# Where a five-layer graph network builds its one-hot matrices, and in which order TensorE uses them

## The chip, the cores and the metric

The kernel runs on one core of a Trainium2 chip. The metric is the time of one execution in microseconds (us) on the device. Before the change the median of three runs is 13644.97 us (13634.25 to 13649.05).

## The reference, cut to what matters

There are 6250 nodes of 64 features and 200000 edges, sorted by destination node. Four graph blocks follow each other; the first has two attention layers, so there are five message-passing layers, called a to e below. Each computes, in its own variant (one or four heads; layers d and e also use one of 8 edge types):

```
score = f(source row[src] , destination row[dst] , edge features)     # one value per edge and head
alpha = exp(score - max over the edges of dst) / sum over the edges of dst
out   = segment_sum(alpha * source row[src], dst)
```

Layers a and b add `edge_attr @ We` (64 features per edge) inside the score, layer c takes the sum of two scalars per head, and layers d and e take dot products. Between the layers stand small dense products and layer norms over the 6250 nodes.

## The kernel before, in words

`prepare` (line 180 and on) computes things that all layers share. Every edge gets the rank of its destination among the destinations that occur; because edges are sorted, the 128 edges of a tile touch only a few neighbouring ranks, so a tile needs one window number and, for each edge, a small rank relative to that window (`rel`, below 256). Then `layer` runs five times: `tables` makes the source rows (to HBM) and the destination rows (`dstW`, in SBUF as three bf16 parts), `stream` walks over all edges, `merge` and `finish` do the rest. Nearly all the time is in `stream`.

`stream` works in groups of 8 tiles of 128 edges, 196 groups in all, and four groups make a chunk (49 chunks). Each engine has its own program, a list of steps, one step per group `u`; engines run in order and meet only at semaphores. The loop over steps is written out for 12 steps (`RING`), and repeats. The two one-hot matrices of a group are:

- `hot` (made by VectorE, `onehot`, L973): 256 ranks on partitions and columns by 1024 edges; it compares a row of relative ranks, loaded by SyncE's queue and spread over the partitions, with the partition's number. TensorE uses it in `expand` to spread destination rows to edges (48 matmuls, six per tile, L1174, and in layers a and b four more for the edge features, L1169).
- `ahot` (made by VectorE, `collect_hot`, L1071): edges on partitions by 256 ranks for each of 8 tiles; it compares `rel` with a table of column numbers, `rankX`. TensorE uses it in `collect` to add the weighted messages by rank (48 matmuls, L1189).

In step `u` the engines do the following; `k = u - LAG` (6 groups behind, 8 in layer d) is the group that is being weighted, and `r = u % 4` is the place in the chunk.

- GpSimd gathers the 1024 source rows of a group with eight indirect DMAs (L914), up to 12 groups ahead of the weighting. SyncE loads indices, ranks, edge features and the chunk's masks.
- VectorE, in this order: `flush(k-2)` adds two PSUM banks to `accS` (L966, waits for `collect(k-2)`); `onehot(u+2)`; the third bf16 part of `k-1` (L1127, signals `low`); where r = 1 `highest_links` (L1009 to L1011); `weigh(k)` (L1062, waits for `alpha` of its chunk), `collect_hot(k)` (L1071), a remainder (L1139); where r = 0 `highest` (L1001 to L1003, the segment maximum by scans, waits for `turned`); where r = 1 `highest_all` (L1018 to L1023, waits for `gaveC`); `score(u)` (L1093 to L1112, waits for `expand(u)` and for the gather).
- TensorE: where r = 1 `give_ends` (L1196), where r = 2 the transposition of the exponentials (L1215); `expand(u+1)`; where r = 0 the transposition of the chunk's scores (`turned`, L1226); where r = 1 `give_carry` (L1203); then `collect(k-1)`, which waits for `low` of `k-1` and for two zeroed PSUM banks.
- ScalarE: sets each PSUM bank to zero after its flush (L929); copies `alpha` from PSUM where r = 2 (L932; in layer d where r = 3, L944); rounds two bf16 parts (L936, L938); where r = 1 the exponential (L941).

Layer d normalises in the stream as well: `total` (r = 2, before `weigh`), `total_links` (r = 2, before the score, waits for a second `give_ends` that TensorE issues after `expand`) and `total_all` (L1048 to L1054, r = 3, before `weigh`, waits for a `give_carry` that TensorE issues before `expand`); its `alpha` needs a matmul that TensorE issues after `expand` of r = 3.

Of the kernel before, what the change touches and what calls it, by code (L numbers as in the profile page):

```python
# [20 lines left out]
ALU = mybir.AluOpType  # L21
# [117 lines left out]
def build(nc, t, out, nlayers=5):  # L139
    with ExitStack() as ctx:  # L140
# [3 lines left out]
        def dram(name, shape, dt=F32):  # L144
# [50 lines left out]
def prepare(nc, t, m, d):  # L195

    with ExitStack() as ctx:
# [68 lines left out]

        MADE = 22

        with nc.Block() as block:
# [25 lines left out]
            def _(g):  # L295
# [18 lines left out]
                for h in range(4):  # L314
# [7 lines left out]
                                base=0, pattern=[[1, P]], channel_multiplier=-1).then_inc(made, 1)  # L322
                g.iota(m["rankX"][:, :, :], pattern=[[1, 2 * P], [0, GROUP]], base=0, channel_multiplier=0,
                       allow_small_or_imprecise_dtypes=True).then_inc(made, 1)
# [3 lines left out]
                       allow_small_or_imprecise_dtypes=True).then_inc(made, 1)  # L328
                g.iota(m["pid"][:, :], pattern=[[P, 2]], base=0, channel_multiplier=1,
                       allow_small_or_imprecise_dtypes=True).then_inc(made, 1)  # L330
# [458 lines left out]
def stream(nc, t, m, d, i, spec, table, dstW):  # L789
# [8 lines left out]
    with ExitStack() as ctx:  # L798
# [12 lines left out]
        hot = [sb(f"hot{s}", [P, 2, GE], BF16) for s in range(2)]  # L811
        ahot = [sb(f"ahot{s}", [P, 2 * P, GROUP], BF16) for s in range(2)]
        mid = [sb(f"mid{s}", [P, GROUP, D]) for s in range(2)]
# [15 lines left out]
        if i == 3:  # L829
# [12 lines left out]
        psA = [ps(f"psA{s}") for s in range(2)]  # L842
        psX, psY = ps("psX"), ps("psY")

# [3 lines left out]
        masked = [sem(f"masked{s}") for s in range(3)]  # L848
        hots, made, took, scored, sch, xch, ready, blank, wl, pch, sub, past = (
            sem(n) for n in ("hots", "made", "took", "scored", "sch", "xch", "ready", "blank", "wl", "pch", "sub", "past"))  # L850
        turned, ended, gaveE, carried, gaveC, lowered, exped, backed, alphad = (
# [22 lines left out]
        with nc.Block() as block:  # L874
# [44 lines left out]
            def _(a):  # L919
                a.wait_ge(ready, 1)  # L920
                for h in range(2):
                    a.activation(psA[h][:, 0:FW * CW], zero[:, :], ACT.Copy).then_inc(zeroed, 1)

                def step(it, s):
                    u, c, r, xc, xs, xq, k, ks = places(it, s)
# [4 lines left out]
                    if i != 3 and r == 2 and within(xc, CHUNKS):  # L930
                        a.wait_ge(backed, xc + 1)
                        a.activation(alpha[xs][:, :, :].rearrange("p h t -> p (h t)"), psY[:, 384:384 + R], ACT.Copy).then_inc(alphad, 1)  # L932
                    if within(k, GROUPS):
# [8 lines left out]
                    if i == 3 and r == 3 and within(xc, CHUNKS):  # L942
                        a.wait_ge(backed, xc + 1)
                        a.activation(alpha[xs][:, 0, :], psY[:, 384:384 + CT], ACT.Copy).then_inc(alphad, 1)  # L944
                rounds(a, step, END)

            @block.vector
            def _(v):
                v.memset(zero[:, :], 0.0).then_inc(ready, 1)
                if i <= 1:  # L950
                    v.memset(we[:, :], 0.0).then_inc(blank, 1)
                v.memset(accS[:, :, :], 0.0).then_inc(xch, 1)
                v.memset(tk[:, :, :], -BIG).then_inc(xch, 1)
                if i == 3:
                    v.memset(tk1[:, :, :], 0.0).then_inc(xch, 1)
                FIRST = 3 if i == 3 else 2
                v.wait_ge(xch, FIRST)

                def flush(k, ks):

                    windows = load_windows(nc, m["win"], k * GROUP, GROUP, mybir.EngineType.DVE, KR - 1)
                    for h in range(2):
# [3 lines left out]
                        v.tensor_tensor(at, at, psA[h][:, 0:FW * CW].rearrange("p (w f) -> p w f", f=CW), ALU.add).then_inc(flushed, 1)  # L966

                def onehot(it, s):
                    g = it * RING + s
                    v.wait_ge(fed[s % 4], it * (3 * FEED) + (s // 4) * FEED + FEED)  # L970
                    wait(v, made, g - 1)
# [22 lines left out]
                given = psY[0:1, 0:2 * (P + 1)].rearrange("a (x n) -> a x n", x=2)[:, :, 0:R - 1]  # L994

# [18 lines left out]
                def highest_all(xc, xs):  # L1014

                    link = linker(xc, 3)
                    v.wait_ge(gaveC, xc + 1)
                    v.tensor_copy(carry[:, :], psY[0:R, 258:260]).then_inc(sub, 1)  # L1018
# [25 lines left out]
                def total_all(xc, xs):  # L1044

                    link = linker(xc, 10)
                    v.wait_ge(gaveC2, xc + 1)
                    v.tensor_copy(carry[:, :], psY[0:R, 258:260]).then_inc(sub, 1)  # L1048
                    v.wait_ge(sub, xc * 2 + 2)
# [64 lines left out]
                def step(it, s):  # L1114
                    u, c, r, xc, xs, xq, k, ks = places(it, s)
                    live = within(xc, CHUNKS)
                    if within(k - 2, GROUPS):
                        flush(k - 2, (ks - 2) % RING)
                    if within(u + 2, GROUPS):
                        if known(u):  # L1120
                            onehot((u + 2) // RING, (u + 2) % RING)
                        else:
                            onehot(it if s + 2 < RING else it + 1, (s + 2) % RING)
                    if within(k - 1, GROUPS):
# [21 lines left out]
                    if within(u, GROUPS):  # L1146
                        score(it, s)
                onehot(0, 0)
                onehot(0, 1)
                rounds(v, step, END)  # L1150

            @block.tensor
            def _(pe):
# [25 lines left out]
                def collect(k, ks):  # L1179
# [3 lines left out]
                    for h in range(2):  # L1183
                        pe.wait_ge(zeroed, k * 2 + (h + 1))
                        for j in range(FL * h, FL * h + FL):
                            w = windows[j]
                            for a in range(2):
                                for part in range(3):
                                    last = pe.matmul(sums[h][a][:, bass.ds(w, 1), :], ahot[ks % 2][:, a * P:(a + 1) * P, j],  # L1189
                                                     parts[ks % 3][:, part, j, :], start=False, stop=False, skip_group_check=True)  # L1190
                        last.then_inc(summed, 1)

                def give_ends(sem_in, value, sem_out):
                    pe.wait_ge(sem_in, value)
                    pe.sem_inc(past, 1)
                    pe.transpose(psY[0:1, 0:R], ends[:, 1:2], m["ident"][0:R, 0:R])  # L1196
                    pe.transpose(psY[0:1, P:P + R], ends[:, 0:1], m["ident"][0:R, 0:R]).then_inc(sem_out, 1)

                def give_carry(sem_in, value, sem_out):
                    pe.wait_ge(sem_in, value)  # L1200
                    pe.sem_inc(past, 1)
                    for x in range(2):
                        last = pe.transpose(psY[0:R, 258 + x:259 + x], car[0:1, x, 0:R], m["ident"][0:1, 0:1])  # L1203
                    last.then_inc(sem_out, 1)

                def step(it, s):
                    u, c, r, xc, xs, xq, k, ks = places(it, s)
                    live = within(xc, CHUNKS)
                    if r == 1 and live:
                        wait(pe, alphad, xc)  # L1210
                        give_ends(ended, xc + 1, gaveE)
                    if i != 3 and r == 2 and live:
                        pe.wait_ge(exped, xc + 1)
                        pe.sem_inc(past, 1)
                        pe.transpose(psY[:, 384:384 + R], Ex[:, :], m["ident"][0:R, 0:R]).then_inc(backed, 1)  # L1215
                    if i == 3 and r == 3 and live:
# [14 lines left out]
                    if i == 3 and r == 3 and live:  # L1231
                        pe.wait_ge(normed, xc + 1)
                        pe.matmul(psY[:, 384:384 + CT], Al[:, :], m["quart"][:, :], start=True, stop=True).then_inc(backed, 1)
# [413 lines left out]
```

## Time and profile before

| what | value |
|---|---|
| median of the runs | 13644.97 us |
| the profiled execution | 13576.47 us, its span 13574.4 us |
| TensorE matmuls | 10504.2 us busy (77%) |
| VectorE | 8519.3 us (63%) |
| ScalarE | 2406.7 us (18%) |
| GpSimd | 9220.1 us (68%) |
| mean granted TensorE clock | 0.573 of full |
| DMA | 912.63 MB, 67 GB/s |

The shares are means over the whole span. The five `stream` stretches fill some 11,080 us of it, `prepare` the first 660 us, and the rest lies between the layers. Inside a stretch every group takes some 11.3 us, so a row of the timeline repeats 196 times with small differences. The chain of waits covers only the last few per cent of the span, so the stretches have to be read from the timeline.

### The profile page before, as it was taken

How to read it: one execution, taken by the hardware profiler on the slowest of the kernel's cores; microseconds unless marked ns; L12 is line 12 of the kernel's file. 1: busy time of each engine (PE TensorE's matmuls, PEld its weight loads, DVE VectorE, ACT ScalarE, POOL GpSimd, SP SyncE). 2: the span in 40 equal slices, each digit the busy share in tenths (PEclk: the TensorE clock that was granted, in tenths of full speed). 3: DMA queues.
4: the chain of work that ended last, by engine and by line, in shares of the span. 5: the costliest groups of instructions: out<-in, count | busy, mean ns of one | idle time of the engine just before them, and what ended most of it. 6: DMA issues, size and time to landing. Idle time of an engine off the chain costs nothing. (4 is left out here: it accounts for less than half of the span.)

```text
span 13574.4 us, 346433 instructions
## 1 busy us (share of the span) xinstructions
PE 10504.2 (77%) x102671; PEld 8732.6 (64%) x102672; DVE 8519.3 (63%) x15786; ACT 2406.7 (18%) x4954; POOL 9220.1 (68%) x8386
## 2 busy tenths in 40 slices
PE   2388888857888888488888857888888578888872
PEld 1377777746777777377777735777777357777762
DVE  7567777755777777355555544777777446666664
ACT  0011212111111122022222211111111112222220
POOL 0177777756777776577777735777777257777761
PEclk9855556555555555555555555555555555555555
DMA  0333333323333332222222223232222233333320
GB/s 16 84 75 71 73 73 73 73 42 75 72 72 73 73 71 57 39 55 54 55 54 55 54 54 106 77 78 77 77 78 72 69 96 78 78 78 78 78 64 11
DMA packets 771899, 912.63 MB, mean 67 GB/s; under 512 B 400125, under 2 KB 447616, under 8 KB 769760
## 3 DMA queue, kind: packets, MB, share of 16 engines
q0 software_dynamic: 267232, 390.16, 15.0%
q1 hardware_dynamic: 503008, 498.92, 13.0%
q8 instruction: 1216, 19.92, 0.6%
q14 instruction: 443, 3.63, 0.1%
HBM read 791.99 MB, written 96.35 MB: 65 GB/s over the span
## 5 line engine op out<-in xcount | busy, mean ns | idle before, releaser
L914 POOL DMA_INDIRECT bs_gat<-table_b,bs_idx x1568 | 1750.7, 1117 | 506.5 <-issue 477.5
L914 POOL DMA_INDIRECT ds_gat<-table_d,ds_idx x1568 | 1749.3, 1116 | 506.7 <-issue 506.7
L914 POOL DMA_INDIRECT as_gat<-table_a,as_idx x1568 | 1740.9, 1110 | 506.6 <-issue 477.5
L914 POOL DMA_INDIRECT es_gat<-table_e,es_idx x1568 | 1725.7, 1101 | 505.6 <-issue 505.6
L914 POOL DMA_INDIRECT cs_gat<-table_c,cs_idx x1568 | 1731.0, 1104 | 491.0 <-issue 491.0
L1174 PE MATMUL ds_psM<-dstW_d,ds_hot 128*128 x9408 | 1252.7, 232 | 194.4 <-DVEq L1107 72.2
L1174 PE MATMUL es_psM<-dstW_e,es_hot 128*128 x9408 | 1253.5, 226 | 175.9 <-issue 65.3
L1174 PE MATMUL cs_psM<-dstW_c,cs_hot 128*128 x9408 | 1232.0, 183 | 182.3 <-DVEq L1100 68.9
L1174 PEld LDWEIGHTS ds_psM<-dstW_d,ds_hot 128*128 128x128 bf16 x9408 | 972.2, 103 | 481.6 <-issue 241.1
L1174 PEld LDWEIGHTS es_psM<-dstW_e,es_hot 128*128 128x128 bf16 x9408 | 962.6, 102 | 480.8 <-issue 224.4
L1174 PEld LDWEIGHTS cs_psM<-dstW_c,cs_hot 128*128 128x128 bf16 x9408 | 967.5, 103 | 473.0 <-issue 223.3
L1174 PE MATMUL as_psM<-dstW_a,as_hot 128*128 x9408 | 997.9, 227 | 4.0
L1174 PE MATMUL bs_psM<-dstW_b,bs_hot 128*128 x9408 | 987.2, 230 | 5.0
L1174 PEld LDWEIGHTS as_psM<-dstW_a,as_hot 128*128 128x128 bf16 x9408 | 861.9, 114 | 182.3 <-issue 9.5
L1174 PEld LDWEIGHTS bs_psM<-dstW_b,bs_hot 128*128 128x128 bf16 x9408 | 862.2, 116 | 176.7 <-issue 12.3
L1189 PE MATMUL bs_psA<-bs_parts,bs_ahot 128*128 128x65 bf16 x9408 | 614.1, 251 | 181.1 <-issue 126.0
L1189 PE MATMUL as_psA<-as_parts,as_ahot 128*128 128x65 bf16 x9408 | 614.4, 251 | 180.6 <-issue 127.5
L1189 PE MATMUL cs_psA<-cs_parts,cs_ahot 128*128 128x68 bf16 x9408 | 613.6, 253 | 174.8 <-issue 161.2
L1189 PE MATMUL es_psA<-es_parts,es_ahot 128*128 128x68 bf16 x9408 | 612.8, 251 | 168.1 <-issue 144.4
L1189 PEld LDWEIGHTS as_psA<-as_parts,as_ahot 128*128 128x128 bf16 x9408 | 588.8, 167 | 211.0 <-issue 210.9
L1189 PEld LDWEIGHTS bs_psA<-bs_parts,bs_ahot 128*128 128x128 bf16 x9408 | 588.5, 167 | 211.3 <-issue 211.2
L1189 PEld LDWEIGHTS cs_psA<-cs_parts,cs_ahot 128*128 128x128 bf16 x9408 | 588.0, 168 | 201.0 <-issue 201.0
(758 smaller groups left out, 17937.2 us busy)
## 6 DMA issues: line engine op xcount, KB each, us to landing
as_rank<-rel_d SPq DMA_DIRECT2D x196, 256.0 KB
as_ea<-in_eaT SPq DMA_DIRECT2D x196, 256.0 KB
bs_rank<-rel_d SPq DMA_DIRECT2D x196, 256.0 KB
bs_ea<-in_eaT SPq DMA_DIRECT2D x196, 256.0 KB
cs_rank<-rel_d SPq DMA_DIRECT2D x196, 256.0 KB, 3.2
ds_rank<-rel_d SPq DMA_DIRECT2D x196, 256.0 KB, 3.3
es_rank<-rel_d SPq DMA_DIRECT2D x196, 256.0 KB, 3.4
table_e<-et_st SPq DMA_DIRECT2D x49, 544.0 KB, 2.7
```

Of the source, the lines that this page charges most:

```text
L914: g_.indirect_dma_start(gat[s][:, j, :], None, table, bass.IndirectOffsetOnAxis(ap=idxS[s][:, j:j + 1].bitcast(U32), axis=0)).then_inc(got ...
L1174: last = pe.matmul(o, hot[s % 2][:, a, j * P:(j + 1) * P], dstAt[a][part][:, bass.ds(w, 1), :], start=(a == part == 0 and i > 1), stop=(a ...
L1189: last = pe.matmul(sums[h][a][:, bass.ds(w, 1), :], ahot[ks % 2][:, a * P:(a + 1) * P, j], parts[ks % 3][:, part, j, :], start=False, stop ...
```

## The change: what it does

1. `hot` moves from VectorE to ScalarE. Instead of one compare per half, ScalarE computes `Square(rank - p)` and then `Relu(1 - square)`: four activations of 128x1024 for a group instead of two VectorE compares. They stand at the end of ScalarE's step, for group `u+2`, and signal the same semaphore.
2. `ahot` is made by eight `tensor_scalar` compares of 128x256, one per tile, which read the column numbers from PSUM (`psI`, fp32) and the tile's ranks as a per-partition scalar (so `rel` becomes fp32). The layout becomes tile by tile. It was one `tensor_tensor` of 128x2048 bf16 in SBUF.
3. `psY` gives its bank to `psI`, and what was in `psY` moves to other columns of `psX`. The wait on `alphad` moves from `give_ends` (r = 1) to the transposition of the scores (r = 0).
4. In TensorE's step `collect(k-1)` comes first; it was last.

```diff
-            rel=sb("rel", [P, TILES], BF16),
+            rel=sb("rel", [P, TILES]),
-            rankX=sb("rankX", [P, 2 * P, GROUP], BF16),
-            pid=sb("pid", [P, 2]),
+            iota=sb("iota", [P, 2 * P]),
+            pidN=sb("pidN", [P, 2]), one=sb("one", [P, 1]),
...
             @block.scalar
+                def onehot(it, s):
+                    g = it * RING + s
+                    a.wait_ge(fed[s % 4], it * (3 * FEED) + (s // 4) * FEED + FEED)
+                    wait(a, made, g - 1)
+                    wait(a, hots, g)
+                    for x in range(2):
+                        a.activation(off[:, x, :], rank[s % 4][:, :], ACT.Square, bias=m["pidN"][:, x:x + 1]).then_inc(apart, 1)
+                    for x in range(2):
+                        a.wait_ge(apart, g * 2 + (x + 1))
+                        last = a.activation(hot[s % 2][:, x, :], off[:, x, :], ACT.Relu, bias=m["one"][:, 0:1], scale=-1.0)
+                    last.then_inc(hots, 1)
                 def step(it, s):
...
                     if i == 3 and r == 3 and within(xc, CHUNKS):
                         a.wait_ge(backed, xc + 1)
-                        a.activation(alpha[xs][:, 0, :], psY[:, 384:384 + CT], ACT.Copy).then_inc(alphad, 1)
+                        a.activation(alpha[xs][:, 0, :], psX[:, 256:256 + CT], ACT.Copy).then_inc(alphad, 1)
+                    if within(u + 2, GROUPS):
+                        onehot((u + 2) // RING, (u + 2) % RING)
...
             @block.vector
+                v.tensor_copy(psI[:, 0:2 * P], m["iota"][:, :]).then_inc(xch, 1)
...
-                def onehot(it, s):
-                    for a in range(2):
-                        last = v.tensor_scalar(hot[s % 2][:, a, :], rank[s % 4][:, :], m["pid"][:, a:a + 1], None, ALU.is_equal)
-                    last.then_inc(hots, 1)
...
-                    v.tensor_tensor(ahot[ks % 2][:, :, :], over(m["rel"][:, bass.ds(k * GROUP, GROUP)], 1, [P, 2 * P, GROUP]),
-                                    m["rankX"][:, :, :], ALU.is_equal).then_inc(ahots, 1)
+                    for j in range(GROUP):
+                        last = v.tensor_scalar(ahot[ks % 2][:, j, :], psI[:, 0:2 * P], m["rel"][:, bass.ds(k * GROUP + j, 1)], None, ALU.is_equal)
+                    last.then_inc(ahots, 1)
...
             @block.tensor
                 def step(it, s):
+                    if within(k - 1, GROUPS):
+                        collect(k - 1, (ks - 1) % RING)
                     if r == 1 and live:
-                        wait(pe, alphad, xc)
                         give_ends(ended, xc + 1, gaveE)
...
                     if r == 0 and live:
                         pe.wait_ge(scored, xc * CG + CG)
-                        wait(pe, lowered, xc)
+                        wait(pe, alphad, xc)
                         pe.transpose(psX[0:R, 0:P], sc[xs][:, :, :].rearrange("p h t -> p (h t)"), m["ident"][:, :]).then_inc(turned, 1)
...
-                    if within(k - 1, GROUPS):
-                        collect(k - 1, (ks - 1) % RING)
```

## Rows read from the trace of the kernel before

**Rows 1.** Stretches by engine (us, then busy us of each): second and fifth layer.

```profile
3157.00:5384.00 2227.00, 1911.77 (x20331) 1677.43 (x20332) 1576.08 (x2835) 429.81 (x852) 1749.52 (x1567) 0.57 0.33 73
...
10968.00:13171.00 2203.00, 1901.20 (x18768) 1558.97 (x18768) 1400.44 (x2642) 446.01 (x852) 1725.00 (x1568) 0.57 0.32 78
```

**Rows 2.** The gathers, one tile (min/median/max ns), first layer.

```profile
L914 POOL DMA_INDIRECT as_gat<-table_a,as_idx x1568: 940/946/3140, 657.1 to 2874.6; - x196
```

**Rows 3.** The page, costliest groups: the same gathers (mean ns, idle before).

```profile
L914 POOL DMA_INDIRECT as_gat<-table_a,as_idx x1568 | 1740.9, 1110 | 506.6 <-issue 477.5
```

**Rows 4.** Timeline (start, length in us), TensorE, first layer.

```profile
2023.80 0.79 PE L1169 MATMUL as_psM<-as_we,as_ea 128*128 128x128 f32 x2 [4.46 <-issue]
...
2030.51 0.37 PE L1226 MATMUL as_psX<-ident,as_sc 128*32 128x128 f32 x1 [0.19 <-issue]
2031.70 3.12 PE L1189 MATMUL as_psA<-as_parts,as_ahot 128*128 128x65 bf16 x48 [0.82 <-issue]
...
2034.94 0.79 PE L1169 MATMUL as_psM<-as_we,as_ea 128*128 128x128 f32 x2
...
2041.41 0.21 PE L1203 MATMUL as_psY<-ident,as_car 1*32 1x1 f32 x2
2042.64 3.12 PE L1189 MATMUL as_psA<-as_parts,as_ahot 128*128 128x65 bf16 x48 [1.01 <-issue]
```

**Rows 5.** Timeline, VectorE, the same stretch.

```profile
2027.02 1.22 DVE L1071 TENSOR_TENSOR as_ahot<-rel,rankX 128x2048 bf16<-128x2048 bf16 x1
...
2031.04 0.41 DVE L1001 TENSOR_TENSOR_SCAN as_A<-as_mk,as_psX 32x128 f32<-32x128 bf16 x1 [2.19 <-PE as_psX L1226]
...
2032.04 0.69 DVE L1093 TENSOR_TENSOR as_mid<-as_psM,as_gat 128x512 f32<-128x512 f32 x1
...
2035.38 0.49 DVE L966 TENSOR_TENSOR as_accS<-as_accS,as_psA 128x325 f32 x1 [0.36 <-issue]
...
2036.50 1.02 DVE L973 TENSOR_SCALAR as_hot<-as_rank,pid 128x1024 bf16<-128x1024 bf16 x2
2037.44 0.69 DVE L1127 TENSOR_TENSOR as_parts<-as_res,as_parts 128x520 bf16<-128x520 f32 x1
2038.05 0.20 DVE L1009 TENSOR_TENSOR as_tk<-as_lk,as_psY 1x62 f32<-1x62 f32 x1
...
2038.54 0.66 DVE L1062 TENSOR_TENSOR as_wtd<-as_gat,as_alpha 128x520 f32<-128x520 f32 x1
...
2041.66 0.15 DVE L1018 COPY as_carry<-as_psY 32x2 f32<-32x2 f32 x1 [0.71 <-PE as_psY L1203]
...
2042.98 0.67 DVE L1093 TENSOR_TENSOR as_mid<-as_psM,as_gat 128x512 f32<-128x512 f32 x1
```

**Rows 6.** Timeline, VectorE, third layer.

```profile
6630.68 0.18 DVE L1099 TENSOR_TENSOR cs_red<-cs_psM,cs_gat 128x32 f32<-128x32 f32 x1
...
6632.03 0.51 DVE L966 TENSOR_TENSOR cs_accS<-cs_accS,cs_psA 128x340 f32 x1 [0.80 <-PE cs_psA L1189]
```

**Rows 7.** Timeline, VectorE, fourth layer.

```profile
9220.39 0.69 DVE L1103 TENSOR_TENSOR ds_mid<-ds_psM,ds_gat 128x512 f32<-128x512 f32 x1 [2.36 <-DMA ds_gat<-table_d,ds_idx]
...
9223.10 0.49 DVE L966 TENSOR_TENSOR ds_accS<-ds_accS,ds_psA 128x320 f32 x1 [1.05 <-issue]
...
9229.55 0.40 DVE L1039 TENSOR_TENSOR ds_tkO<-ds_lkO,ds_psY 1x254 f32<-1x254 f32 x1
...
9230.33 0.39 DVE L1041 TENSOR_TENSOR_SCAN ds_car<-ds_lkO,ds_tkO 1x128 f32<-1x128 f32 x1
...
9236.92 0.14 DVE L1048 COPY ds_carry<-ds_psY 128x2 f32<-128x2 f32 x1
...
9239.22 0.68 DVE L1062 TENSOR_TENSOR ds_wtd<-ds_gat,ds_alpha 128x512 f32<-128x512 f32 x1
```

**Rows 8.** Groups by line, ScalarE (busy us, mean ns).

```profile
L929 ACT ACTIVATE cs_psA<-cs_zero 128x340 f32<-128x340 f32 x392 | 179.4, 458 | 1058.2 <-DVE cs_accS L966 1058.2
...
L938 ACT ACTIVATE cs_parts<-cs_res 128x544 bf16<-128x544 f32 x196 | 128.7, 656 | 203.1 <-DVE cs_res L1139 203.1
...
L941 ACT ACT_TABLE_LOAD x4 | 5.1, 1283 | 0.1
```

**Rows 9.** Groups by line, VectorE, operands in PSUM.

```profile
L966 DVE TENSOR_TENSOR as_accS<-as_accS,as_psA 128x325 f32 x392 | 193.5, 494 | 165.4 <-issue 94.3 <-DVE as_accS L966 36.7 <-PE as_psA L1189 33.8
...
L712 DVE COPY bt_st<-bt_psA 128x64 f32<-128x64 f32 x49 | 11.0, 225 | 39.3 <-DMA table_b<-bt_st 38.3 <-PE bt_psD L784 1.0
```

More of the change, by code:

```diff
@@ L265, in prepare @@
         LOADS = 10
-        MADE = 22
+        MADE = 23
         with nc.Block() as block:
@@ L322, in _ @@
                                 base=0, pattern=[[1, P]], channel_multiplier=-1).then_inc(made, 1)
-                g.iota(m["rankX"][:, :, :], pattern=[[1, 2 * P], [0, GROUP]], base=0, channel_multiplier=0,
+                g.iota(m["iota"][:, :], pattern=[[1, 2 * P]], base=0, channel_multiplier=0,
                        allow_small_or_imprecise_dtypes=True).then_inc(made, 1)
@@ L328, in _ @@
                        allow_small_or_imprecise_dtypes=True).then_inc(made, 1)
-                g.iota(m["pid"][:, :], pattern=[[P, 2]], base=0, channel_multiplier=1,
+                g.memset(m["one"][:, :], 1.0).then_inc(made, 1)
+                g.iota(m["pidN"][:, :], pattern=[[-P, 2]], base=0, channel_multiplier=-1,
                        allow_small_or_imprecise_dtypes=True).then_inc(made, 1)
@@ L811, in stream @@
         hot = [sb(f"hot{s}", [P, 2, GE], BF16) for s in range(2)]
-        ahot = [sb(f"ahot{s}", [P, 2 * P, GROUP], BF16) for s in range(2)]
+        off = sb("off", [P, 2, GE], BF16)
+        ahot = [sb(f"ahot{s}", [P, GROUP, 2 * P], BF16) for s in range(2)]
         mid = [sb(f"mid{s}", [P, GROUP, D]) for s in range(2)]
@@ L842, in stream @@
         psA = [ps(f"psA{s}") for s in range(2)]
-        psX, psY = ps("psX"), ps("psY")
+        psX, psI = ps("psX"), ps("psI")
         fed = [sem(f"fed{s}") for s in range(4)]
@@ L848, in stream @@
         masked = [sem(f"masked{s}") for s in range(3)]
-        hots, made, took, scored, sch, xch, ready, blank, wl, pch, sub, past = (
-            sem(n) for n in ("hots", "made", "took", "scored", "sch", "xch", "ready", "blank", "wl", "pch", "sub", "past"))
+        hots, made, took, scored, sch, xch, ready, blank, wl, pch, sub, past, apart = (
+            sem(n) for n in ("hots", "made", "took", "scored", "sch", "xch", "ready", "blank", "wl", "pch", "sub", "past", "apart"))
         turned, ended, gaveE, carried, gaveC, lowered, exped, backed, alphad = (
@@ L931, in step @@
                         a.wait_ge(backed, xc + 1)
-                        a.activation(alpha[xs][:, :, :].rearrange("p h t -> p (h t)"), psY[:, 384:384 + R], ACT.Copy).then_inc(alphad, 1)
+                        a.activation(alpha[xs][:, :, :].rearrange("p h t -> p (h t)"), psX[:, 256:256 + R], ACT.Copy).then_inc(alphad, 1)
                     if within(k, GROUPS):
@@ L943, in step @@
                         a.wait_ge(backed, xc + 1)
-                        a.activation(alpha[xs][:, 0, :], psY[:, 384:384 + CT], ACT.Copy).then_inc(alphad, 1)
+                        a.activation(alpha[xs][:, 0, :], psX[:, 256:256 + CT], ACT.Copy).then_inc(alphad, 1)
+                    if within(u + 2, GROUPS):
+                        if known(u):
+                            onehot((u + 2) // RING, (u + 2) % RING)
+                        else:
+                            onehot(it if s + 2 < RING else it + 1, (s + 2) % RING)
+                onehot(0, 0)
+                onehot(0, 1)
                 rounds(a, step, END)
@@ L955, in _ @@
                     v.memset(tk1[:, :, :], 0.0).then_inc(xch, 1)
-                FIRST = 3 if i == 3 else 2
+                FIRST = 4 if i == 3 else 3
                 v.wait_ge(xch, FIRST)
@@ L966, in flush @@
                         v.tensor_tensor(at, at, psA[h][:, 0:FW * CW].rearrange("p (w f) -> p w f", f=CW), ALU.add).then_inc(flushed, 1)
-                def onehot(it, s):
-                    g = it * RING + s
-                    v.wait_ge(fed[s % 4], it * (3 * FEED) + (s // 4) * FEED + FEED)
-                    wait(v, made, g - 1)
-                    for a in range(2):
-                        last = v.tensor_scalar(hot[s % 2][:, a, :], rank[s % 4][:, :], m["pid"][:, a:a + 1], None, ALU.is_equal)
-                    last.then_inc(hots, 1)
                 XL = {0: 5, 1: 5, 2: 5, 3: 13, 4: 5}[i]
@@ L993, in neighbours @@
                     return take.rearrange("a (x n) -> a x n", x=2)[:, :, 0:R - 1]
-                given = psY[0:1, 0:2 * (P + 1)].rearrange("a (x n) -> a x n", x=2)[:, :, 0:R - 1]
+                given = psX[0:1, P:P + 2 * (P + 1)].rearrange("a (x n) -> a x n", x=2)[:, :, 0:R - 1]
                 def highest(xc, xs, xq):
@@ L1017, in highest_all @@
                     v.wait_ge(gaveC, xc + 1)
-                    v.tensor_copy(carry[:, :], psY[0:R, 258:260]).then_inc(sub, 1)
+                    v.tensor_copy(carry[:, :], psX[0:R, 400:402]).then_inc(sub, 1)
                     v.wait_ge(sub, (xc + 1) * (2 if i == 3 else 1) - (1 if i == 3 else 0))
@@ L1047, in total_all @@
                     v.wait_ge(gaveC2, xc + 1)
-                    v.tensor_copy(carry[:, :], psY[0:R, 258:260]).then_inc(sub, 1)
+                    v.tensor_copy(carry[:, :], psX[0:R, 400:402]).then_inc(sub, 1)
                     v.wait_ge(sub, xc * 2 + 2)
@@ L1118, in step @@
                         flush(k - 2, (ks - 2) % RING)
[L1119 to L1123, printed above, removed]
                     if within(k - 1, GROUPS):
@@ L1147, in step @@
                         score(it, s)
-                onehot(0, 0)
-                onehot(0, 1)
                 rounds(v, step, END)
@@ L1188, in collect @@
                                 for part in range(3):
-                                    last = pe.matmul(sums[h][a][:, bass.ds(w, 1), :], ahot[ks % 2][:, a * P:(a + 1) * P, j],
+                                    last = pe.matmul(sums[h][a][:, bass.ds(w, 1), :], ahot[ks % 2][:, j, a * P:(a + 1) * P],
                                                      parts[ks % 3][:, part, j, :], start=False, stop=False, skip_group_check=True)
@@ L1195, in give_ends @@
                     pe.sem_inc(past, 1)
-                    pe.transpose(psY[0:1, 0:R], ends[:, 1:2], m["ident"][0:R, 0:R])
-                    pe.transpose(psY[0:1, P:P + R], ends[:, 0:1], m["ident"][0:R, 0:R]).then_inc(sem_out, 1)
+                    pe.transpose(psX[0:1, P:P + R], ends[:, 1:2], m["ident"][0:R, 0:R])
+                    pe.transpose(psX[0:1, 2 * P:2 * P + R], ends[:, 0:1], m["ident"][0:R, 0:R]).then_inc(sem_out, 1)
                 def give_carry(sem_in, value, sem_out):
@@ L1202, in give_carry @@
                     for x in range(2):
-                        last = pe.transpose(psY[0:R, 258 + x:259 + x], car[0:1, x, 0:R], m["ident"][0:1, 0:1])
+                        last = pe.transpose(psX[0:R, 400 + x:401 + x], car[0:1, x, 0:R], m["ident"][0:1, 0:1])
                     last.then_inc(sem_out, 1)
@@ L1214, in step @@
                         pe.sem_inc(past, 1)
-                        pe.transpose(psY[:, 384:384 + R], Ex[:, :], m["ident"][0:R, 0:R]).then_inc(backed, 1)
+                        pe.transpose(psX[:, 256:256 + R], Ex[:, :], m["ident"][0:R, 0:R]).then_inc(backed, 1)
                     if i == 3 and r == 3 and live:
@@ L1232, in step @@
                         pe.wait_ge(normed, xc + 1)
-                        pe.matmul(psY[:, 384:384 + CT], Al[:, :], m["quart"][:, :], start=True, stop=True).then_inc(backed, 1)
-                    if within(k - 1, GROUPS):
-                        collect(k - 1, (ks - 1) % RING)
+                        pe.matmul(psX[:, 256:256 + CT], Al[:, :], m["quart"][:, :], start=True, stop=True).then_inc(backed, 1)
                 if i <= 1:
```

## The prediction

> **What bounds the kernel now.** First the stretches: the five `stream` layers take 2203 to 2227 us each, for 196 groups or 49 chunks [rows 1]. That all five are alike, though VectorE has 1576 us of work in one and 1400 in another, says that VectorE's amount of work does not set the pace. Their sum is 11,078 us, so 226.1 us for one chunk of each layer, 45.2 us a chunk, 11.3 us a group. Then the groups by line: GpSimd issues gathers without a pause, 1.110 us each with 0.32 us between, although the median gather takes 0.946 [rows 2, 3]. Eight at 1.43 us are 11.4 us, the pace. Then the timeline of TensorE, which is almost as full. `expand` starts at 2034.94 and the next `collect` at 2042.64, of which 0.2 are two small transpositions: 7.5 us from one to the other. From the start of `collect` (2031.70) to the next `expand` are 3.2 us. The cycle is 10.7 us, plus an idle time of 4.46 us where the 12-step loop wraps, which is once in 12 groups (0.36 us a group): 11.06 us. TensorE could therefore follow only 2% faster [rows 4].
>
> What counts for this change is a third view, the same stretch on VectorE beside TensorE: who hands what to whom inside a step. Where r = 0, VectorE stands 2.19 us until the scores are transposed, and the scans start 0.53 us after that matmul; where r = 1 it stands 0.71 us for the carry [rows 4, 5]. These waits are short because `expand`, behind which both transpositions are queued, is the first thing in TensorE's step.
>
> **The changed order of TensorE (the main term).** `collect(k-1)` waits for `low`, which VectorE makes in the same step, right after the flush. With `collect` first, everything that TensorE gives VectorE in that step comes after it, and the next step's `low` comes after VectorE has used it. This closes a loop through both in-order queues. I measure each step from the start of one `collect` (0) to the start of the next, in layer a, with these pieces. TensorE: `collect` to `expand` 3.2; `expand` start to transposed scores 6.71 (2023.80 to 2030.51); `expand` to carry 6.47 (2034.94 to 2041.41) [rows 4]. VectorE: scan 0.53 after that; `highest` 1.00 (2031.04 to 2032.04); score to the next flush 3.34 (2032.04 to 2035.38); flush to the third part 2.06, without the two compares that leave (0.94) 1.12; the part 0.69; 0.15 for the signal: 1.96 together [rows 5].
>
> - r = 0: 3.2 + 6.71 + 0.53 + 1.00 + 3.34 + 1.96 = 16.75 us. VectorE's own work before the scans is hidden in it.
> - r = 1: `ends` now come behind `collect`, at 3.3; the links end at 3.8 (0.49); weighting, compares and remainder (4.0, below) end at 7.8 and wait for the carry: 3.24 + 6.47 + 0.25 = 9.95. Then 1.32 to the score (2041.66 to 2042.98), 3.34 and 1.96: 16.6 us [rows 5].
> - r = 2: the first group of a chunk is weighted here, and its `alpha` is transposed behind `collect` (3.05 + 0.4) and copied by ScalarE (0.3): VectorE starts at 3.85. With 4.0, 3.34 and 1.96 it is 13.25; ScalarE's queue, below, makes it 13.45 us.
> - r = 3: nothing is exchanged, TensorE's cycle of 10.7 us decides.
>
> The sum is 57.5 us. A third of a wrap, now on that path (4.3 / 3 = 1.4), makes 58.9 against 45.2. Layer b is the same.
>
> **The compares from PSUM.** One instruction of 1.22 us and the two `hot` compares (0.94) leave VectorE [rows 5]; eight of 128x256 from PSUM come. No row shows that form. Reads from PSUM take 0.225 us for 64 elements and 0.494 for 325 [rows 9]; on the line between them 256 take 0.42, and following ones overlap by some 0.08 (the weighting's 0.6 for a row of 0.69), so 8 x 0.345 = 2.75 us. Weighting 0.6 and remainder 0.65 give the 4.0 above. The bounds are 8 x 0.145 = 1.2 and 8 x 0.41 = 3.3. It is behind waits for TensorE in r = 0 and 1, and decides in r = 2 or in layer d in r = 3 only: -380 to +135 us over the kernel.
>
> **The one-hots on ScalarE.** ScalarE takes 0.656 us for 544 elements and 0.458 for 340 [rows 8]. I take 1.05 for 1024, 4.2 us a group; bounds are 0.656 and, in proportion, 1.24 each (2.6 and 4.95). Its amount of work is no limit: 430 us of a stretch are busy [rows 1], and 820 more come. But the four stand at the end of its step, and the zeroing of the PSUM bank (0.45), for which the next `collect` waits, is queued behind. r = 2: the second part ends at 8.65, + 4.2 + 0.45 + 0.1 = 13.4. In r = 1 the exponential ends at 11.7, which gives 16.45, just hidden in layer a.
>
> **The other layers.** c: its score is short, 1.35 us to the flush [rows 6], instead of 3.34. r = 0 is 14.85; r = 1 would be 14.7, but ScalarE gives 16.55; r = 2 likewise 13.8; r = 3 10.7; sum with the wrap 57.3. e: I take d's 2.71 [rows 7]: 16.1 + 16.55 + 13.8 + 10.7 + 1.4 = 58.6. d: r = 0 16.1, r = 1 16.55. r = 2: `ends` of the sums come after `expand` (10.1), links 1.17, score and flush 2.71, 1.96: 16.1 with 0.1 for a signal. r = 3: `total_all` (2.30) starts behind `collect` at 3.4, with 4.0 more VectorE is at 9.8; ScalarE rounds, copies `alpha` (10.85), and only then makes the one-hots: + 4.2 + 0.45 + 0.1 = 15.6. The wrap is half hidden there (0.7). Sum 65.0 [rows 7].
>
> **The rest.** `psI` is filled once a layer. The moved `alphad` wait asks for something that was done a chunk ago (r = 2, in layer d r = 3). The one-hots are ready in time: `hot(u+2)` ends before the next `collect`, `expand` needs it 3.2 us later. SyncE loads ranks when `hots` of three groups before is there, as before.
>
> **Sum.** 58.9 + 58.9 + 57.3 + 65.0 + 58.6 = 298.7 us against 226.1 for one chunk of each layer: +72.6 x 49 = 3557 us. On the profiled execution's 13,576 that is 17,133; the median of the runs lies 0.5% above that execution, so I predict 17,200 us.
>
> **A rule that speaks for the change.** The gathers take 0.946 us at the median and 1.110 in the mean, and up to 3.14 [rows 2, 3], so something holds some of them up. The Trainium skill ("SBUF — State Buffer", section "SBUF: two separate sides") says that VectorE and GpSimd share one pair of SBUF ports under an exclusive lock, held by a VectorE instruction that uses both ports, and that descriptors of a DMA issued by GpSimd cannot be written meanwhile. By that rule the instructions that leave VectorE here are among those that held the gathers, and it makes rival A.
>
> **Rivals.**
>
> A, faster: the gathers get back to 0.946 us, 0.164 less each or 1.3 us a group, and the loop above does not form, so TensorE's 11.06 us is the pace: (11.3 - 11.06) x 980 groups = 235 us less, 13,400. For it: gathers do set the pace now. Against: it decides only while VectorE waits for gathers at its score, and in the loop the score waits for the transposition. 5%.
>
> B, no change: the loop costs about what the gathers give back. It would need 1 us of stall in a chunk, where I count 12. 2%.
>
> C, slower still: ScalarE must load a function table between the exponential and the square. One load is 1.283 us, now four for this line in the whole kernel [rows 8], since copy and exponential share one. Two a chunk are 2.57 x 245 = 630 us at most: 17,800. 10%. The Trainium skill ("ScalarE: Activation LUTs", section "Table sets: the hidden batching unit") says that cheap functions are in every set; by that there is none.
>
> D, slower by less: only one of the two long steps is stretched, since an instruction of the loop starts earlier than I read; half of the 3557 us, 15,400. 5%.
>
> **How the numbers follow.** The forecast has 78%. Its range is 16,500 (both unknown durations at their low ends, ScalarE's worth -310) to 17,700 (+350 and +135); with most of C and a little of D it is 16,400 to 17,900. A measurement of this kernel tells about 0.2% from no change: slower by over 0.2% has 93%, within 0.2% has 2%, faster by over 0.2% has 5%.
>
> **What would show it.** In the profile after: a group of 14 to 16 us; TensorE idle before `collect` by 5 us and more in two of four steps, ended by VectorE's `parts` (L1127's line) or ScalarE's zeroing; VectorE idle before the scans by 5 us and more, ended by `psX`; gathers near 0.95 us, with pauses, that end on `weighted` or are not on the path; ScalarE near 6.6 us a group. Wrong would be: an unchanged wait of about 2 us before the scans; TensorE at 10.7 us in all four steps (A); table loads by the hundred (C).

## The result and the profile after

The changed kernel takes 16885.18 us (median of 4 runs, 16883.75 to 16890.68), the kernel before beside it 13647.01 us: 1.238 times as long, interval 1.235 to 1.240. The profiled executions have spans of 16883.6 and 13574.4 us, 3309 us apart. I had predicted 3557 us more than the profiled execution before, and 17,200 for the median. The forecast was right: slower, and inside the range of 16,500 to 17,700.

The page of the changed kernel, busy time, share of the span and instructions, then four of its costliest groups (busy, mean ns, idle before and its releaser):

```profile
PE 10254.3 (61%) x102671; PEld 8411.5 (50%) x102672; DVE 9629.8 (57%) x20691; ACT 6366.2 (38%) x8874; POOL 8190.8 (49%) x8387
...
L916 POOL DMA_INDIRECT as_gat<-table_a,as_idx x1568 | 1553.3, 991 | 1243.4 <-DMA as_idx<-in_srcT 533.8
...
L1198 PE MATMUL as_psA<-as_parts,as_ahot 128*128 128x65 bf16 x9408 | 553.0, 244 | 937.1 <-DVE as_parts L1138 475.0
L1198 PE MATMUL es_psA<-es_parts,es_ahot 128*128 128x68 bf16 x9408 | 570.7, 247 | 904.0 <-ACT es_psA L944 469.0
L1198 PE MATMUL bs_psA<-bs_parts,bs_ahot 128*128 128x65 bf16 x9408 | 553.0, 244 | 924.4 <-ACT bs_psA L944 460.3
```

Every engine but ScalarE, which got the one-hots (38%, it was 18%), has a lower share than before. Against [rows 3] a gather is faster (0.991 us, it was 1.110), and GpSimd now stands idle for 1243 us in layer a instead of 507. What ended TensorE's idle time before `collect` is VectorE's third part (L1138) or ScalarE's zeroing (L944). The stretches of layers b and e, to be held against [rows 1] (length, then busy us of TensorE, its weight loads, VectorE, ScalarE and GpSimd, granted clock, DMA share, GB/s):

```profile
3780.00:6617.00 2837.00, 1865.77 (x20429) 1609.27 (x20430) 1799.13 (x3797) 1228.16 (x1643) 1537.19 (x1568) 0.57 0.25 57
13663.00:16495.00 2832.00, 1874.13 (x18918) 1523.89 (x18918) 1631.65 (x3624) 1241.05 (x1648) 1530.57 (x1568) 0.55 0.25 61
```

Both are over 600 us longer, with less TensorE time in them than before and nearly the same granted clock (0.57 and 0.55, against 0.57 in both). No engine has become the bound; waits have. The timeline of TensorE in layer a shows them (start, length, idle before), beside [rows 4]:

```profile
2031.44 2.82 PE L1198 MATMUL as_psA<-as_parts,as_ahot 128*128 128x65 bf16 x48 [5.07 <-issue]
2034.67 0.54 PE L1178 MATMUL as_psM<-as_we,as_ea 128*128 128x128 f32 x2 [0.41 <-issue]
...
2041.36 0.37 PE L1236 MATMUL as_psX<-ident,as_sc 128*32 128x128 f32 x1
2048.47 2.82 PE L1198 MATMUL as_psA<-as_parts,as_ahot 128*128 128x65 bf16 x48 [6.74 <-DVE as_parts L1138]
...
2058.20 0.18 PE L1212 MATMUL as_psX<-ident,as_car 1*32 1x1 f32 x2
2065.16 2.82 PE L1198 MATMUL as_psA<-as_parts,as_ahot 128*128 128x65 bf16 x48 [6.78 <-ACT as_psA L944]
```

and VectorE in the same 34 us, beside [rows 5]:

```profile
2041.87 0.41 DVE L1016 TENSOR_TENSOR_SCAN as_A<-as_mk,as_psX 32x128 f32<-32x128 bf16 x1 [8.95 <-PE as_psX L1236]
...
2046.31 0.49 DVE L989 TENSOR_TENSOR as_accS<-as_accS,as_psA 128x325 f32 x1 [0.37 <-issue]
...
2047.43 0.69 DVE L1138 TENSOR_TENSOR as_parts<-as_res,as_parts 128x520 bf16<-128x520 f32 x1
2051.52 0.21 DVE L1024 TENSOR_TENSOR as_tk<-as_lk,as_psX 1x62 f32<-1x62 f32 x1 [3.39 <-PE as_psX L1206]
...
2052.62 3.21 DVE L1087 TENSOR_SCALAR as_ahot<-as_psI,rel 128x256 bf16<-128x256 f32 x8
...
2058.42 0.15 DVE L1033 COPY as_carry<-as_psX 32x2 f32<-32x2 f32 x1 [1.98 <-PE as_psX L1212]
```

One turn of the loop reads: `collect` at 2031.44, scores transposed at 2041.36 behind `expand`, scans at 2041.87 after 8.95 us of standing, the third part at 2047.43, the next `collect` at 2048.47. While VectorE stands, TensorE works, and then TensorE stands (6.74 us) while VectorE works. The next turn is the same over the ends and the carry (3.39 and 1.98 us of standing).

### The profile page after: what moved, and what is told of

It reads as the page before. It is cut to its first block and busy times, and to the rows that moved or that the text cites. A ratio compares the mean times of both kernels' runs of the same rounds, so it can differ in the third digit from the quotient of the medians.

```text
span 16883.6 us, 364359 instructions
## 1 busy us (share of the span) xinstructions
PE 10254.3 (61%) x102671; PEld 8411.5 (50%) x102672; DVE 9629.8 (57%) x20691; ACT 6366.2 (38%) x8874; POOL 8190.8 (49%) x8387
## 3 DMA queue, kind: packets, MB, share of 16 engines
q0 software_dynamic: 267232, 390.16, 11.8%
q1 hardware_dynamic: 503008, 498.92, 10.5%
## 5 line engine op out<-in xcount | busy, mean ns | idle before, releaser
L916 POOL DMA_INDIRECT ds_gat<-table_d,ds_idx x1568 | 1526.3, 973 | 1580.1 <-DVE ds_wtd L1077 934.9
L916 POOL DMA_INDIRECT as_gat<-table_a,as_idx x1568 | 1553.3, 991 | 1243.4 <-DMA as_idx<-in_srcT 533.8
L916 POOL DMA_INDIRECT bs_gat<-table_b,bs_idx x1568 | 1537.2, 980 | 1245.3 <-DMA bs_idx<-in_srcT 516.5
L916 POOL DMA_INDIRECT es_gat<-table_e,es_idx x1568 | 1530.7, 976 | 1227.2 <-issue 574.0
L916 POOL DMA_INDIRECT cs_gat<-table_c,cs_idx x1568 | 1524.5, 972 | 1160.8 <-issue 544.0
L1198 PE MATMUL ds_psA<-ds_parts,ds_ahot 128*128 128x64 bf16 x9408 | 538.8, 242 | 1196.5 <-DVE ds_parts L1138 729.1
L1198 PEld LDWEIGHTS ds_psA<-ds_parts,ds_ahot 128*128 128x128 bf16 x9408 | 507.2, 130 | 1246.0 <-issue 1244.8
L1198 PEld LDWEIGHTS as_psA<-as_parts,as_ahot 128*128 128x128 bf16 x9408 | 522.2, 132 | 967.6 <-issue 967.4
L1198 PEld LDWEIGHTS es_psA<-es_parts,es_ahot 128*128 128x128 bf16 x9408 | 537.3, 133 | 936.7 <-issue 934.9
L1198 PEld LDWEIGHTS bs_psA<-bs_parts,bs_ahot 128*128 128x128 bf16 x9408 | 521.8, 132 | 955.3 <-issue 954.8
```

Of the source, the lines that this page charges most:

```text
L916: g_.indirect_dma_start(gat[s][:, j, :], None, table, bass.IndirectOffsetOnAxis(ap=idxS[s][:, j:j + 1].bitcast(U32), axis=0)).then_inc(got ...
```

## The experiments

Each ratio is against the kernel before on the same chip; the runs fell on several chips, so kernels are compared by ratio. "Steps" are the times from the start of one `collect` to the next, as medians for r = 0, 1, 2, 3 over the groups of a layer, its first and last 12 left out. Before they are 11.0 / 10.8 / 10.7 / 10.9 us in layer a, changed 16.6 / 16.9 / 13.2 / 10.7.

**Order alone.** The kernel before, with this edit and nothing else:

```diff
                 def step(it, s):
+                    if within(k - 1, GROUPS):
+                        collect(k - 1, (ks - 1) % RING)
                     if r == 1 and live:
...
-                    if within(k - 1, GROUPS):
-                        collect(k - 1, (ks - 1) % RING)
```

> The kernel before with only TensorE's collect moved to the front of its step; both one-hots stay on VectorE as they were. Theory: r = 0 and r = 1 take 16 to 17.6 us, now with VectorE's two hot compares (0.94 us) on the path from flush to low, r = 2 about 12 us, r = 3 10.7 us, 17 and 13.7 us for r = 2 and 3 in layer d; about 296 us for one chunk of each layer, 16,600 to 17,000 us in all, as slow as the changed kernel. Rival (ScalarE's queue and the compares carry a good part of the loss): under 15,500 us.

Measured: 16987.14 us, ratio 1.255 (1.253 to 1.257); steps in layer a 17.5 / 17.6 / 12.3 / 11.7. Its waits (us in all, times, longest):

```profile
PE ds_psA L1189 <- DVE ds_parts L1127: 1230.2, 196, 8.3
...
PE bs_psA L1189 <- DVE bs_parts L1127: 926.6, 182, 8.9
```

The order by itself costs more than the whole change (1.238). With the order given, the rest of the change wins about 1.4% back (a ratio of ratios from two chips).

**Collect last.** The changed kernel with that edit undone.

> The changed kernel with TensorE's collect put back to the end of its step; one-hots on ScalarE and compares from PSUM stay. Theory (the order makes the loop through turned, gaveE, gaveC and alpha): the four steps of a chunk are all 10.7 us again, the wait before the scans is 1 to 3 us, and TensorE's pace of 10.7 us plus a third of a us for the wrap decides: 13,300 to 13,500 us, 0.975 to 0.99 of the kernel before. Rival (the 4.2 us of ScalarE before the zeroing, or the 3.1 us of compares, make the stall): 15,000 us or more.

Measured: 13891.05 us, ratio 1.026 (1.025 to 1.027). Most of the loss is gone, but my number was missed: layer a has steps of 11.0 / 12.6 / 10.6 / 10.8 and layer d 10.9 / 13.0 / 10.7 / 13.6. The timeline shows the late one, first ScalarE, then TensorE:

```profile
2053.63 0.31 ACT L956 ACTIVATE as_Ex<-as_Dx 32x128 f32<-32x128 f32 x1 [0.67 <-DVE as_Dx L1038]
2053.84 2.17 ACT L933 ACTIVATE as_off<-as_rank,pidN 128x1024 bf16<-128x1024 bf16 x2
2055.92 2.17 ACT L936 ACTIVATE as_hot<-as_off,one 128x1024 bf16<-128x1024 bf16 x2
```

```profile
2052.80 2.82 PE L1198 MATMUL as_psA<-as_parts,as_ahot 128*128 128x65 bf16 x48 [1.06 <-issue]
2058.15 0.49 PE L1178 MATMUL as_psM<-as_we,as_ea 128*128 128x128 f32 x2 [2.35 <-ACT as_hot L936]
```

Where r = 1, the one-hots stand on ScalarE behind the exponential, and that waits for the carry. They end at 2058.1, and `expand`, due at 2055.8, waits 2.35 us.

**ScalarE's one-hots alone.** The kernel before with edit 1 only.

> The kernel before with the two wide one-hots made by ScalarE at the end of its step, and nothing else changed: the compares that place the groups' columns stay on their old operands, the collect stays last. Theory (late ScalarE one-hots are the cost that is left with the collect last): 13,750 to 13,900 us, with 12 us or more in the step after the one-hots. Rival (the PSUM compares are the cost): 13,400 to 13,550, level with the kernel before.

Measured: 13814.11 us, ratio 1.016 (1.015 to 1.018), the step of r = 1 at 12.5 to 12.8 us in all layers, the others 10.5 to 11.0 but for r = 3 of layer d (11.8). As the theory had it.

**PSUM compares alone.** The changed kernel with the collect last and `hot` back on VectorE:

```diff
-                        a.activation(off[:, x, :], rank[s % 4][:, :], ACT.Square, bias=m["pidN"][:, x:x + 1]).then_inc(apart, 1)
...
+                        last = v.tensor_scalar(hot[s % 2][:, a, :], rank[s % 4][:, :], m["pidN"][:, a:a + 1], 0.0, ALU.add, ALU.is_equal)
```

> The changed kernel with the collect last and the wide one-hots back on VectorE: what is left of the change is the compares with the column numbers in PSUM, eight a group at 0.40 us apiece. Theory (the compares cost nothing that is not hidden; VectorE has some 3 us of idle time in a group of 11): 13,450 to 13,600 us. Rival (the compares are the cost): 13,800 or more, VectorE busy over 10.5 us of each group.

Measured: 13565.62 us, ratio 0.998 (0.997 to 0.999). That the compares cost little holds, for the sum. They win a little in four layers (10.9 to 11.1 us a group over the whole layer, from 11.1 to 11.2) and lose in layer d (11.8 from 11.2), where the steps of r = 1, 2 and 3 are 11.8 / 12.1 / 12.6; what holds that layer was not followed up. The gathers in the pages of these two, ScalarE's one-hots alone first:

```profile
L918 POOL DMA_INDIRECT as_gat<-table_a,as_idx x1568 | 1740.6, 1110 | 506.9 <-issue 472.1 <-DMA as_idx<-in_srcT 32.0 <-DVE as_wtd L1078 2.7
```

```profile
L916 POOL DMA_INDIRECT as_gat<-table_a,as_idx x1568 | 1574.8, 1004 | 595.5 <-issue 464.5 <-DMA as_idx<-in_srcT 130.3 <-DVE as_wtd L1065 0.6
```

Taking the two 128x1024 compares off VectorE left the gather at 1.110 us [rows 3]; replacing the one 128x2048 compare by eight from PSUM brought it to 1.004. So in layer a it was that instruction that held gathers up. The trace of the kernel before says the same: in layer a the 349 gathers that overlap it take 1.46 us in the mean, the other 1219 take 1.01. The 189 that also overlap the remainder behind it (L1139) take 1.77. A long gather overlaps more for being long, so the run without the instruction is the stronger evidence. Where they do not meet it, they are not held: in the run with exchanges first on the one-hots of before (last of the experiments, on a slow chip), only 2 gathers of layer a overlap the same instruction, and the mean is 0.981 us.

**One-hots between the roundings.** Collect last, and ScalarE's order changed:

```diff
                         a.activation(parts[ks % 3][:, 0, :, :], wtd[ks % 2][:, :, :], ACT.Copy).then_inc(high, 1)
+                    if within(u + 2, GROUPS):
...
+                        onehot(*ahead)                            # two squares, first Relu
+                    if within(k, GROUPS):
                         a.wait_ge(rest, k + 1)
                         a.activation(parts[ks % 3][:, 1, :, :], res[ks % 2][:, :, :], ACT.Copy).then_inc(middle, 1)
+                    if within(u + 2, GROUPS):
+                        half(ahead[0] * RING + ahead[1], ahead[1], 1)   # second Relu
                     if r == 1 and within(xc, CHUNKS):
...
-                    if within(u + 2, GROUPS):
-                        if known(u):
-                            onehot((u + 2) // RING, (u + 2) % RING)
```

> The changed kernel with the collect back at the end of TensorE's step, and ScalarE's squares and first Relu moved between its two roundings, the second Relu behind them. Theory (with the collect last, what is left of the loss, 13,891 us, is ScalarE's one-hots arriving late in one step of four: 12.6 us against 10.7 there): the step falls back to 10.7 to 11.2 us, the time to 13,450 to 13,600 us, level with the kernel before (about 13,540). Rival (the loss is the traffic of VectorE's added compares, 3.22 us a group): it stays at 13,800 to 13,900. Rival 2 (the moved one-hots now delay ScalarE's roundings): over 13,900. On a chip where the kernel before needs 18,200 us instead, TensorE's pauses hide all of it and every time lies within 2% of that.

Measured: 13398.39 us, ratio 0.986 (0.984 to 0.987). Steps are 11.0 / 10.7 / 10.7 / 10.9 in layer a, and the time is below the expected band. This version beats the kernel before by 1.4%. TensorE in it:

```profile
2039.86 2.82 PE L1205 MATMUL as_psA<-as_parts,as_ahot 128*128 128x65 bf16 x48 [0.80 <-issue]
2043.09 0.76 PE L1185 MATMUL as_psM<-as_we,as_ea 128*128 128x128 f32 x2 [0.23 <-DMA as_rank<-rel_d]
...
2050.85 2.82 PE L1205 MATMUL as_psA<-as_parts,as_ahot 128*128 128x65 bf16 x48 [0.98 <-issue]
2054.11 0.60 PE L1185 MATMUL as_psM<-as_we,as_ea 128*128 128x128 f32 x2 [0.20 <-DMA as_rank<-rel_d]
...
2061.50 2.82 PE L1205 MATMUL as_psA<-as_parts,as_ahot 128*128 128x65 bf16 x48 [0.88 <-issue]
```

No wait in these 25 us is over 1 us, and TensorE's own cycle is the pace. The median steps are those of the kernel before to 0.1 us; what fell is the mean step of layer a, from 11.37 to 11.18 us. So the gain lies in the steps that had waited, not in a shorter cycle.

**Exchanges first.** The changed kernel, with TensorE's step in another order:

```diff
                 def step(it, s):
+                    if r == 0 and live:
+                        pe.wait_ge(scored, xc * CG + CG)
...
-                    if within(k - 1, GROUPS):
-                        collect(k - 1, (ks - 1) % RING)
                     if r == 1 and live:
                         give_ends(ended, xc + 1, gaveE)
...
+                    if within(k - 1, GROUPS):
+                        collect(k - 1, (ks - 1) % RING)
...
+                    if within(u + 1, GROUPS):
...
```

Every exchange that stood behind `collect` now stands ahead of it or between `collect` and `expand` (the carry, and in layer d the second ends and the matmul for `alpha`).

> The changed kernel, still with collect ahead of expand, but each exchange with VectorE as early as its input allows: the transpositions of scores, ends and exponentials ahead of collect, the carry and the second ends between collect and expand. Theory (what costs is that the exchanges are queued behind collect and expand, not that collect is ahead of expand): no wait of VectorE over 3 us in a step, TensorE's 10.7 us pace, 13,250 to 13,500 us. Rival (collect ahead of expand costs by itself, since expand then starts only after low, so the score waits for it): 14,000 us or more.

Measured: 13451.36 us, ratio 0.994 (0.992 to 0.995). Here `collect` may come before `expand`, as long as what VectorE waits for does not stand behind both. With ScalarE's one-hots between the roundings as well:

> The version with the exchanges ahead of the collect, which took 13,451 us, and ScalarE's one-hots between its two roundings as well. Theory: little is left to win, since TensorE waited only some 40 us a layer for a ScalarE one-hot there; 13,380 to 13,470 us. Rival (the one-hots between the roundings delay the parts that the collect reads): 13,550 to 13,800.

Measured: 13406.66 us, ratio 0.986 (0.985 to 0.988), inside the expected band and level with the version above.

**Scores first.** The changed kernel with only the transposition of r = 0 ahead of `collect`.

> The changed kernel with one of its two loops undone: the transposition of the chunk's scores (r = 0) goes ahead of the collect, all else, the carry and the ends of r = 1 too, stays behind it. Theory (each exchange behind the collect stretches its own step): the step of r = 0 falls from 16.6 us to about 10.8 (in layer c from 14.9), the steps of r = 1 (16.5 to 16.9) and, in layer d, of r = 2 and 3 stay. That is 5.8 + 5.9 + 4.0 + 5.3 + 5.2 = 26 us for one chunk of each layer, 1,280 us in 49 chunks: 15,500 to 15,700 us. Rival (the long steps are one stretch caused by the collect's place, and the transposition ahead only moves the wait to the next step): 16,500 to 16,900. Rival 2 (TensorE's order matters only for the scores): 13,900 to 14,100, the time with the collect last.

Measured: 20148.56 us, ratio 1.107 (1.105 to 1.109) on a chip where the kernel before took 18195.22. The forecast of 15,500 to 15,700 us missed. In layers a and b the step of r = 0 fell to 10.6 and 10.8 as expected, but that of r = 1 rose to some 25 us; in c, d and e r = 0 was 22 to 24 us. It does not settle what one loop costs by itself, because something else stretches every kernel there (last section).

**A chip that is slow for every kernel.** The version with one-hots between, the one with exchanges first as well, and ScalarE's one-hots alone had run before on such a chip, with the exchanges-first order on the one-hots of before as a fourth. For that one:

> The kernel before, its one-hots as they were, with TensorE's step as exchanges whose input is there, collect, remaining exchanges, expand. Theory (the gathers, at 1.11 us while VectorE makes both one-hots from SBUF, set the pace again): 13,450 to 13,650 us, no different from the kernel before by over 0.5%. Rival (the order is what gains, not the one-hots): 13,400 us or less.

Measured there: before 18188.97 us, and ratios 0.996, 1.013, 1.001 and 1.007 (18303.93 us). The first three had been expected at 13,200 to 13,400, 13,250 to 13,420 and 13,750 to 13,900 us, and like the fourth they missed there. Repeated, the same files, on an ordinary chip they were 0.986, 0.986 and 1.016 (13,398, 13,407 and 13,814 us), inside those bands. The fourth was not repeated, so whether the new order without the new one-hots wins anything stays open.

## Why the prediction was right, and where it was off

**What bounds the kernel.** Right. The mean pace was set by gathers with TensorE just behind. In the best version the gathers are at 0.98 to 0.995 us, eight with their 0.3 between are under 10.4, and median steps stay at 10.5 to 11.0 but in layer d (up to 11.5). The 1.4% won is rival A's mechanism (2% was its limit); A failed as a forecast because the loop did form.

**The loop.** Right, step by step, within 0.5 us, for r = 0, 1, 2, 3 (medians in us):

| layer | predicted | measured |
|---|---|---|
| a | 16.75 / 16.6 / 13.45 / 10.7 | 16.60 / 16.88 / 13.16 / 10.65 |
| b | as a | 16.85 / 16.71 / 13.12 / 10.68 |
| c | 14.85 / 16.55 / 13.8 / 10.7 | 14.86 / 16.48 / 13.33 / 10.48 |
| d | 16.1 / 16.55 / 16.1 / 15.6 | 16.18 / 16.52 / 16.10 / 15.19 |
| e | 16.1 / 16.55 / 13.8 / 10.7 | 16.06 / 16.58 / 13.33 / 10.64 |

With the wraps a chunk of each layer is 297.5 us (means), predicted 298.7. Rival D (only one long step) is refuted by the table, rival B by the result. One sum is off by 0.1: the pieces of r = 2 in layer a give 13.15 us, not 13.25; ScalarE's 13.45 decides there, so nothing follows from it. In r = 1 I had ScalarE's queue just hidden in layers a and b. It is not: of the 43 such steps in the middle of a layer, the wait of the next `collect` ends with ScalarE's zeroing in 28 in layer a and in all 43 in layer b. The size came out right because the two paths lie so close (16.6 and 16.45 us predicted), which is partly luck.

**Where the 248 us went.** The over-estimate has three parts. The chunks are 1.2 us too long in my sum, 57 us in 49 of them. I subtracted 226.1, the mean of whole stretches, where the middle of the layers had 227.1: 50 us. The rest, some 140 us or 28 a layer, is the step "x 49". From the first `collect` of a layer to its last the five layers grew by 3357 us, so the first and last groups, which lack part of the exchanges, did not grow in proportion; outside these stretches the kernel became 48 us shorter. The term that was mis-sized is that factor, not a duration.

**Durations that no row had shown.** In the groups by line of the changed kernel:

```profile
L936 ACT ACTIVATE as_hot<-as_off,one 128x1024 bf16<-128x1024 bf16 x392 | 425.6, 1132 | 0.0
...
L956 ACT ACT_TABLE_LOAD x4 | 5.1, 1283 | 0.1
...
L1087 DVE TENSOR_SCALAR as_ahot<-as_psI,rel 128x256 bf16<-128x256 f32 x1568 | 630.5, 473 | 0.0
```

ScalarE's activation takes 1.13 us, two of them 2.17, so 1.05 apart was near enough. The PSUM compare takes 0.473, and eight 3.21 us, not 2.75: near the upper bound, since I put one at 0.42 and read too much overlap out of the weighting. It stays inside waits in r = 0 and 1: in the turn above VectorE still stands 1.98 us for the carry after it. The table loads are four, as before: rival C is refuted. The Trainium skill ("ScalarE: Activation LUTs", "Table sets: the hidden batching unit") says that cheap functions are in every set. The trace agrees, for the square too, which that section does not name.

**The gathers.** 0.99 us instead of 1.110, with pauses; I had written near 0.95. The Trainium skill ("SBUF — State Buffer", "SBUF: two separate sides") has the shared ports held by a VectorE instruction in a two-port mode, or by one with two inputs in SBUF while GpSimd reads SBUF. The runs agree in part. The compare of 128x2048 has two inputs in SBUF and held gathers. The remainder has two as well, yet with the PSUM compares alone the 120 gathers of layer a that meet it and not the compares take 0.944 us. The 128x1024 compares, one input each, cost little: gathers of the kernel before that meet them and neither of the other two take 1.04 us in layer a, against 1.00 for those that meet none of the three. Without them the mean gather stayed at 1.110 in layer a and fell by 0.02 to 0.06 us in the others. Which property of the instruction holds a gather stays open.

**A step that was wrong though it cost nothing here.** "The one-hots are ready in time" holds in the changed order, where `expand` comes 3.2 us after a late `collect`. With the collect last it fails where r = 1, for 1.6% by itself and, with the PSUM compares, 2.6%; the two edits meet in layer d, where each alone takes 11.6 and 11.8 us a group and both together 12.0. I had not put ScalarE's exponential ahead of the one-hots in that chain.

## What to carry to other kernels

When work is moved inside an in-order step, list for every result that another engine waits for what now stands ahead of it, and follow that engine back to what it owes the first one: if that comes later in its own queue, the two take turns, and the step costs the sum of both. The cure is to put the tiny handovers (here matmuls of 0.2 to 0.4 us) ahead of the large blocks; the order of the blocks themselves then cost nothing here (ratio 0.994). Work handed to an idle engine belongs ahead of the instruction in its queue that waits longest; here that turned 1.026 into 0.986.

## What the runs showed of the hardware

The same kernel file (one-hots between the roundings) took 13398.39 us on one chip and 18112.95 on another, where the kernel before took 18188.97. The pages of the two executions for the same 9408 matmuls, the slow chip first:

```profile
L1205 PE MATMUL as_psA<-as_parts,as_ahot 128*128 128x65 bf16 x9408 | 659.9, 242 | 780.5 <-issue 744.8
```

```profile
L1205 PE MATMUL as_psA<-as_parts,as_ahot 128*128 128x65 bf16 x9408 | 553.7, 245 | 186.2 <-issue 149.6
```

One matmul takes the same 0.24 us (mean granted clock 0.528, on the ordinary chip 0.576), but TensorE pauses before many of them with nothing that it waits for. The timeline of the slow one shows single matmuls between pauses:

```profile
2401.51 0.22 PE L1205 MATMUL as_psA<-as_parts,as_ahot 128*128 128x65 bf16 x1 [1.06 <-issue]
2402.24 0.21 PE L1205 MATMUL as_psA<-as_parts,as_ahot 128*128 128x65 bf16 x1 [0.51 <-issue]
2402.96 2.53 PE L1205 MATMUL as_psA<-as_parts,as_ahot 128*128 128x65 bf16 x43 [0.51 <-issue]
```

Starts of neighbouring matmuls that lie 0.6 to 0.8 us apart are 2647 in it and 236 on the ordinary chip. What causes them was not found. Ratios measured in such a condition (0.996) do not carry over (0.986).

Weight loads of `collect` from the new, tile by tile layout take 0.133 us at the median, from the old one 0.170 (ScalarE's one-hots alone, with the old layout, has 0.169; PSUM compares alone 0.133), and 48 matmuls of `collect` 2.82 us instead of 3.12 [rows 4]. I had not counted that, but little of it reaches the cycle: from the start of `collect` to the start of the next `expand` are 3.30 us at the median in layer a of the kernel before, and 3.21 with the one-hots between the roundings.
